# Post-LN transformer layer: the first weights go ahead of the first x

## The reference

```python
r = sigmoid(x @ Wr.T); k = x @ Wk.T; v = x @ Wv.T
scale = exp(t * log(sigmoid(decay)))              # per position and feature
state = cumsum(k * v / clip(scale, 1e-10)) * scale
y = rmsnorm(r * state, ln_w) @ Wo.T
x = layernorm(x + y)
h = gelu(x @ binarize(w1).T + b1)                 # 256 -> 1024
x = layernorm(x + h @ binarize(w2).T + b2)
```

## Time and profile before

| | |
|---|---|
| median of 3 runs | 842.73 us (842.6 to 844.2) |
| profiled execution, its own time | 842.26 us |
| its span, first to last instruction | 840.5 us |
| TensorE busy | 809.7 us, 96% |
| VectorE busy | 754.3 us, 90% |
| ScalarE busy | 678.0 us, 81% |
| GpSimd busy | 356.5 us, 42% |

### The profile page before, as it was taken

One profiled execution on the slowest core, in us unless ns is written; L12 is line 12 of the kernel. 1 busy time (PEld: TensorE's weight loads), 2 busy tenths in 40 slices (PEclk: granted clock), 3 DMA queues, 4 the chain that ended last, 5 costly groups with the idle time before them and its releaser, 6 DMA issues.

```text
span 840.5 us, 16849 instructions
## 1 busy us (share of the span) xinstructions
PE 809.7 (96%) x5351; PEld 524.9 (62%) x5351; DVE 754.3 (90%) x1399; ACT 678.0 (81%) x969; POOL 356.5 (42%) x579
## 2 busy tenths in 40 slices
PE   5888999999999999999999999999999999999995
PEld 3455666666666666666666666666666666666553
DVE  4889999999999999999999999999999999999876
ACT  5886888888888888888888888888888888888674
POOL 5684333443333444333344333344433334433444
PEclk9999999999999999999999999999999999999998
DMA  8304535344543443553434554334355343444322
GB/s 247 78 28 101 126 89 93 96 109 115 125 107 92 91 108 100 125 125 83 108 84 103 122 125 107 93 89 110 100 125 125 81 106 88 103 97 101 76 51 75
DMA packets 169845, 86.27 MB, mean 103 GB/s; under 512 B 130144, under 2 KB 165472, under 8 KB 169824
## 3 DMA queue, kind: packets, MB, share of 16 engines
q1 hardware_dynamic: 148304, 52.97, 27.4%
q0 software_dynamic: 4608, 16.78, 10.3%
q10 hardware_dynamic: 16912, 16.26, 5.7%
HBM read 20.45 MB, written 16.78 MB: 44 GB/s over the span
## 4 chain that ended last, share of the span: by engine, by line
PE 85%; DVE 6%; POOL 4%; ACT 2%; issue 2%; DMA 1%; POOLq 0%; ACTq 0%; DVEq 0%; SPq 0%
PE ps_r L355 26%; PE ps_o L473 24%; PE ps_f L428 18%; PE ps_r L428 6%; PE ps_o L382 6%; PE ps_o L387 3%; PE ps_s L362 2%; POOL clip_g L1315 1%; DMA x_in<-in_L_attn_x_dram 1%; DVE hid_lo L957 1%; DMA x_t<-x_st 1%; POOL u_rstd L1246 1%; ACT res L666 0%; DVE state L880 0%; DVE u L906 0%
## 5 line engine op out<-in xcount | busy, mean ns | idle before, releaser
L473 PE MATMUL ps_o<-w2T,hid_hi 128*128 128x256 f16 x992 | 218.8, 273 | 6.1 <-DVE hid_lo L957 5.7
L473 PE MATMUL ps_o<-w2T,hid_lo 128*128 128x256 f16 x992 | 218.8, 273 | 0.0
L355 PE MATMUL ps_r<-x_t,proj_hi 128*128 128x512 f16 x768 | 197.1, 379 | 4.1 <-DVE proj_lo L1038 1.4
L648 ACT ACTIVATE hid<-ps_f,b1c,f_scale 128x512 f32<-128x512 f32 x192 | 145.2, 774 | 50.8 <-PE ps_f L428 45.6
L428 PE MATMUL ps_f<-x_t,w1T 128*128 128x512 f16 x768 | 181.9, 379 | 1.1 <-DMA x_t<-x_st 0.9
L1231 POOL TENSOR_TENSOR y_sqs<-y_sq 128x512 f32<-128x512 f32 x32 | 46.8, 1462 | 300.9 <-ACT y_sq L623 300.9
L957 DVE SCALAR_TENSOR_TENSOR hid_lo<-hid,hid_scale,hid_hi 128x1024 f16<-128x1024 f32 (+1 forms) x136 | 161.0, 1227 | 1.6 <-POOL hid_hi L1256 1.6
L355 PEld LDWEIGHTS ps_r<-x_t,proj_hi 128*128 128x128 f16 x768 | 74.7, 98 | 93.6 <-issue 5.2
L685 ACT ACTIVATE hid_hi<-hid,hid_scale 128x2048 f16<-128x2048 f32 (+2 forms) x70 | 125.7, 1797 | 3.2
L428 PEld LDWEIGHTS ps_f<-x_t,w1T 128*128 128x128 f16 x768 | 75.1, 98 | 79.1 <-DMA x_t<-x_st 1.2
L355 PE MATMUL ps_r<-x_t,proj_lo 128*128 128x512 f16 x384 | 114.2, 379 | 0.0
(11 more groups left out here) (173 smaller groups left out, 1421.2 us busy)
## 6 DMA issues: line engine op xcount, KB each, us to landing
x_in<-in_L_attn_x_dram SPq DMA_DIRECT2D x32, 512.0 KB, 3.8
res<-b_row POOLq DMA_DIRECT2D x32, 512.0 KB, 4.6
out_dram<-res ACTq DMA_DIRECT2D x31, 512.0 KB, 3.1
w_in<-in_L_ffn_w_dram SPq DMA_DIRECT2D x2, 1024.0 KB, 9.9
x_t<-x_st SPq DMA_TRANSPOSE x59, 4.3
b_row<-in_L_ffn_b_dram SPq DMA_DIRECT2D x1, 512.0 KB, 13.6
proj_in<-in_L_attn_Wk_dram SPq DMA_DIRECT2D x1, 256.0 KB, 5.1
proj_in<-in_L_attn_Wv_dram SPq DMA_DIRECT2D x1, 256.0 KB, 5.3
```

Of the source, the lines that this page charges most:

```text
L355: last = nc.tensor.matmul(ps_r[:, m, :], w[:, m, dc, ec * P:(ec + 1) * P], xx[:, :, dc, :], start=(n == 0), stop=(n == 3 * DC - 1))
L473: last = nc.tensor.matmul(o_tok[:, tt, :], hh[:, hc, tt * P:(tt + 1) * P], w2T[:, :, hc, :], start=(hc == 0 and n == 0), stop=(hc == HC - ...
L648: nc.scalar.activation(hid[:, hc, :], f1_bank[hc % NF], ACT.Gelu, bias=b1c[:, hc:hc + 1], scale=f1_scale[:, hc:hc + 1]).then_inc(s_gelu, 1)
```

## The change

SyncE loads Wk and Wv first, then chunk 0's x, then Wr. TensorE transposes the first two weights and sums their maxima before it transposes x, and the third weight after; the transposes of the identity become 24 in place of 4. The first products of chunk 0, m = 0 and m = 1, run one behind the other, and the sum of the third weight's maxima stands ahead of them. ScalarE computes the Ln before `xsq` of chunk 0 and splits the first two weights before it writes `xh`. VectorE takes all three maxima ahead of x's bound and the third weight's scale, and splits the first two weights before `xl`.

```diff
--- before.py
+++ after.py
@@ -262,8 +262,9 @@
             sp.sem_inc(s_xt, 16)
             sp.sem_inc(s_x1t, 16)
             sp.sem_inc(s_zadd, 1)
-            load(0, 0, 0)
             for n, w in enumerate((Wk, Wv, Wr)):
+                if n == 2:
+                    load(0, 0, 0)
                 sp.dma_start(proj_in[:, n], w.rearrange("(c p) d -> p c d", p=P)).then_inc(s_proj_in[n], 16)
             load(1, 0, 1)
             sp.dma_start(wo_in[:, :, :], Wo.rearrange("(c p) d -> p c d", p=P)).then_inc(s_wo_in, 16)
@@ -528,22 +529,20 @@
 
             def prologue():
                 pe.wait_ge(s_ident, 1)
+                proj_transposes(0)
+                sum_wmax(ps_wmax[:, 0:1], 0, 1, 1)
+                proj_transposes(1)
+                pe.wait_ge(s_wscl, 1)
+                sum_wmax(ps_wmax[:, 1:2], 1, 1, 2)
                 TX(0, 0, 0, True)
+                pe.wait_ge(s_wscl, 2)
                 sum_xbound(0)
-                for n in range(3):
-                    proj_transposes(n)
-                    if n == 0:
-                        pe.wait_ge(s_xtmp, 1)
-                        sum_wmax(ps_wmax[:, 0:1], 0, 1, 1)
-                    if n == 1:
-                        pe.wait_ge(s_wscl, 1)
-                        sum_wmax(ps_wmax[:, 1:2], 1, 1, 2)
-                for n in range(TT):
+                proj_transposes(2)
+                pe.wait_ge(s_xtmp, 1)
+                sum_wmax(ps_wmax[:, 2:3], 2, 1, 3)
+                for n in range(6 * TT):
                     nc.tensor.transpose(ps_f[:, 1, 0:P], ident[:, :], ident[:, :])
-                R(0, True, looped=False, ecs=(0,), ms=(0,))
-                pe.wait_ge(s_wscl, 2)
-                sum_wmax(ps_wmax[:, 2:3], 2, 1, 3)
-                R(0, True, looped=False, ecs=(0,), ms=(1,))
+                R(0, True, looped=False, ecs=(0,), ms=range(2))
                 pe.wait_ge(s_wscl, 3)
                 sum_xbound(1)
                 R(0, True, looped=False, ecs=(0,), ms=(2,))
@@ -692,10 +691,9 @@
                           allow_slow_non_contiguous=True).then_inc(s_lnw_in, 16)
             act.wait_ge(s_decay_in, 16)
             nc.scalar.activation(dec_c[:, 1, :], dec_c[:, 0, :], ACT.Sigmoid).then_inc(s_setup_a, 1)
-            xsq(0, 0, 0, first=True)
             act.wait_ge(s_setup_v, 1)
             nc.scalar.activation(dec_c[:, 2, :], dec_c[:, 1, :], ACT.Ln).then_inc(s_setup_a, 1)
-            xh(0, 0)
+            xsq(0, 0, 0, first=True)
             def proj_split_hi(n):
                 act.wait_ge(s_setup_pe, n + 1)
                 act.wait_ge(s_wscl, n + 1)
@@ -744,6 +742,7 @@
             def prologue():
                 proj_split_hi(0)
                 proj_split_hi(1)
+                xh(0, 0)
                 act.wait_ge(s_setup_a, 2)
                 act.wait_ge(s_const, 1)
                 clip_table(0)
@@ -1043,15 +1042,15 @@
             dve.wait_ge(s_decay_in, 16)
             dve.wait_ge(s_setup_a, 1)
             nc.vector.tensor_scalar_max(dec_c[:, 1, :], dec_c[:, 1, :], CLIP_DEC).then_inc(s_setup_v, 1)
-            take_xbound(0, 0)
             for n in range(2):
                 proj_maximum(n)
                 proj_scale(n)
-            xl(0, 0)
+            proj_maximum(2)
+            take_xbound(0, 0)
+            proj_scale(2)
             proj_split_lo(0)
             proj_split_lo(1)
-            proj_maximum(2)
-            proj_scale(2)
+            xl(0, 0)
             dve.wait_ge(s_wscl, 3)
             nc.vector.tensor_scalar_mul(w_inv[:, 2:3], w_inv[:, 2:3], 0.5).then_inc(s_winv, 1)
             proj_split_lo(2)
```

## The result

The changed kernel takes 846.18 us (median of 9 runs; 841.98 to 847.21), the kernel before 842.73. The ratio is 1.0031, interval 1.0019 to 1.0044: slower by 3.45 us, where the prediction had 842.2 and a range to 844.0.

The account below looks back on a forecast made before the run. TensorE, 96% busy, was taken to set the time from about 69 us on; the third product 0.5 us earlier, passed on whole to the end, gave 842.2 from 842.73, range 840.9 to 844.0.

Parts of the forecast that it names:

- a change that ends before that can only shift the whole rest: From about 69 us on TensorE sets the time, so an earlier change only moves everything behind it.
- the line on the fillers: 24 filler transposes on TensorE before the first product: 2.6 us at full clock, costing nothing; 5.2 at half, done at 15.5.
- my rivals: A: gain about 1.0, 841.7, chance 0.25; B: own line; C: nothing arrives at the end, 842.7, chance 0.22.
- B: Fillers at half clock hold up the first product on TensorE; at most +3.7, 846.4; chance 0.08.
- Landings: Loads at the start: x(0) lands at 7.6, some 1.45 later; Wv about 6.14, Wk 4.9.
- the 0.3 that I allowed: x(0) could land 0.3 earlier or later if the queue were unequal over its engines.
- Clock of TX: x(0)'s eight transposes on TensorE end at 8.6 (full clock) or 9.45 (half); 9.35 taken, close to half.
- ScalarE's chain: On ScalarE, from `xh` to the square of chunk 1: 4.52 us after the change, 6.4 before.
- The third product: Chunk 0's m = 2 product on TensorE, on which the start hangs: at 16.48 in place of 16.98, 0.5 us earlier.
- Passing on of the start: The 0.5 gained at the third product stays the same at 24.91 and at the end.
- of fixed time: Between 24.91 and 68.67 us nothing in the views waits for a load of fixed time, so no gain is lost.

Follow-up runs that it names:

- repeated run: The changed kernel measured once more with no edit: 846.38 us, ratio 1.0041; its profiled execution took 848.42.
- count without time: Kernel before plus 20 one-column bf16 products on TensorE ahead of x's landing: 845.12 us, ratio 1.0029.
- time without count: 3 fp32 products of 512 columns as fillers, replacing 24 transposes in the changed kernel (842.43 us) and 4 in the kernel before (843.31 us).
- another place with a higher count: Changed kernel, its 24 fillers kept, plus 14 one-column bf16 products ahead of Wk's landing: 843.46 us, ratio 1.0004.
- the first profile: The first profiled execution of the changed kernel, unedited, the fastest of its nine runs: 841.98 us, span 840.2.
- 20 more pairs: 20 products with their weight loads more than the kernel before: it with bf16 products 845.12 us, it with 24 fillers 847.34, the changed kernel again 846.38.
- the loads alone: Kernel before with only the new order of loads (Wk, Wv, x, Wr): 844.46 us, ratio 1.0019.
- bf16 products: Kernel before plus one-column bf16 products on TensorE ahead of x's landing: 10 gave 843.10 us, 20 gave 845.12, 34 gave 843.09.
- 4 fillers: Changed kernel with 4 filler transposes in place of 24: 843.62 us, ratio 1.0005.
- long fillers: Changed kernel with 3 fp32 products of 512 columns as fillers in place of 24 transposes: 842.43 us, ratio 0.9992.

## Why the prediction was wrong

*The step that failed* is in its first paragraph: "a change that ends before that can only shift the whole rest", and with it the line on the fillers, costed by their time alone ("nothing, the wait for `xl` hides them"). The rest isn't shifted only. 20 more instructions and weight loads move TensorE's fetches, and near 790 us one of them meets the issue of the last transposing load. The issue takes 2.4 to 3.1 us in place of 1.32, the load lands 2 us later, and TensorE, for which the wait was 0.93 already, waits 2.7 to 2.9, in two of three profiles with half clock behind. In the repeated run this place alone costs 3.7 of the 5.5 us. That the count of fillers costs and not their time is shown by count without time (845.12), time without count (842.43 and 843.31) and another place with a higher count (843.46). Instructions and weight loads were always added together, so which of the two counts is not shown.

The same meeting occurs at 142 us, where the load has slack: 2.95 us of issue in the profile after (1.32 before), with no cost there, and 0.27 in the repeated run (3.06). And at the first transposing load of a chunk, at 71 us, a fetch before the landing costs 0.8. None of my rivals had it. B, on the fillers, named the right lines with the wrong mechanism.

That it is the fetch that holds up the load is argued from where the two stand in the profiles; no run moves the fetch alone. The profiles go far together. The seventeen have 1003 transposing loads into `x_t`. Twelve of their issues took 2.15 to 3.14 us, where the others took 1.3 to 2.1, and in all twelve a fetch came 0.29 to 0.77 us behind their start. Only one other issue had a fetch there, the one at 789.90 above. Of the 952 loads with no fetch between issue and landing, none landed later than 4.72 us. The edge isn't understood: 0.75 passed at 790 us, 0.71 to 0.77 didn't at 142, and an issue at 142.12 with a fetch at 143.05 took 1.32, but landed after 5.2 us. The Trainium skill (Runtime: NRT & Kernel Launch, "Instruction fetch mechanics") says that an engine's instruction memory is refilled in blocks of 16 KiB, 256 instructions, over a DMA queue. The trace agrees: a packet of 0.02 MB in the instruction queue, and 40 instructions change its place.

That the first profile came so near the forecast (841.98 for 842.2) is luck: x landed 0.65 us sooner than forecast, and the fetch at its last transposing load passed, where those of the three other profiles with 20 more pairs didn't.

*Landings:* right. x at 7.6 by forecast; its transposes started at 7.66 with the loads alone and at 6.99, 7.42, 7.65, 7.65, 7.90, 7.97 and 8.08 in the kernels with the change. The scatter, 1.1 us, is more than the 0.3 that I allowed. In the kernel before it isn't small either: x landed at 5.54 to 6.26 in its variants with the old order of loads.

*Clock of TX:* right in kind. x's eight transposes ran at half clock in all but the first profile (1.97 in the repeated run, from the first start to the last end).

*ScalarE's chain:* 4.42 for 4.52 (by the rows 4.51) and 4.43 in the repeated run. The third product, forecast at 16.48, is at 15.41 in the first profile, 17.34 in the second, and 16.94, 16.88, 16.61 and 16.19 in four later kernels with the change. The mean of the six is 16.56, 0.4 ahead of 16.98 where I had 0.5. That isn't a measured gain: in the kernel before with bf16 products the third product was at 16.32 to 16.73 too.

*Rival B in its size:* in the repeated run the fillers end at the first product (14.72) and the third is at 17.34, 0.36 later than in before. But with 4 fillers it is at 17.79: the first product comes at 13.61 and runs at half clock (1.87 for four in place of 1.02). With long fillers and x landed at the same time (7.60 and 7.61) the third is at 16.61. The 20 more fillers repay at the start what they cost there.

*Passing on of the start:* right to 0.03 us from chunk 0 to chunk 2 in all profiles, and wrong for chunk 3, where I had seen nothing "of fixed time". There the late landing alone took 0.8 (three profiles), half clock alone 0 to 0.6 (four), both together 0.7 to 1.2 (five).

What the change itself is worth, off the meeting, is 842.43 against 842.76 of the kernel before, run beside it: 0.3 us, and not to be told from nothing. I had 0.5.

## What to carry to other kernels

Count what an edit adds to an engine's instruction stream, apart from its time. In a kernel where one load is awaited without slack (here the last transposing load, 0.93 us late already), a shift of the fetch can cost more than the edit gains, far from the edit; three long fillers did the work of 24 short ones without it. When one profile lies at the edge of the measured times, take a second before explaining, and compare the two by an instruction that comes once in each chunk.

## What the runs showed of the hardware

- An issue of a transposing load on SP near 790 us took 1.32 us, and 2.40, 2.78 and 3.14 with an instruction fetch 0.29, 0.45 and 0.53 us into it; over all 1003 such loads the twelve longest issues (2.15 to 3.14) are those with a fetch 0.29 to 0.77 us into them, save one that stayed 1.32 with a fetch at 0.75. With the fetch 0.31 to 0.35 ahead it stayed 1.32, and took 1.54 with both at once.
- A fetch behind the issue and ahead of the landing often went with a late landing, not always: at 790 us 5.3 and 5.4 us after the issue and not 4.6, with the fetch 2.25 and 2.33 behind it; at 67 us 5.8 to 6.0 and not 4.3 in eight profiles with the fetch 3.8 to 3.9 behind, but 4.6 in two others with 3.81 and 3.82.
- A one-column product took 0.21 us an instruction in fp32 (two instructions, 8.69 for 20 products) and 0.035 in bf16 (0.70 for 20).
- At the same idle of 2.9 us of TensorE, in the 15 profiles where it wasn't filled, the granted clock stayed at 1.00 in 6, was at 0.50 for 3.4 us in 7 and for 6.8 us in 2. The fall came in the idle or up to 1.4 us behind its end.
